# Layer 1: the feed-forward product of a chunk moved among the query heads of a later chunk

## The reference

```python
x = x + _L1_attn_ref(_L1_cond_ref(x, cond), ...)
#   _L1_cond_ref: film of a normed x, 16-head attention of head size 16, W_out
#   _L1_attn_ref: layer norm, 16 query heads of size 128 over one rotated key and value, causal, Wo
x = x + _L1_ffn_ref(_L1_cond2_ref(x, cond), w_fc, w_proj)
#   _L1_cond2_ref: causal depthwise convolution over all 32 lags, taps from cond
h = jnp.maximum(turbo_linear(x, w_fc), 0.0)      # 256 -> 1024
return turbo_linear(h * h, w_proj)               # 1024 -> 256
```

## Time and profile before

| | |
|---|---|
| median of 3 runs | 1476.55 us (1473.99 to 1476.77) |
| profiled execution, span | 1472.0 us |
| PE busy | 1345.4 us, 91% |
| DVE busy | 1101.3 us, 75% |
| ACT busy | 867.2 us, 59% |
| POOL busy | 136.4 us, 9% |
| chain that ended last | PE 49%, DVE 33%, ACT 9%, issue 6% |
| layer 1, steps 1 to 8 | from about 966 us to the end |

### The profile page before, as it was taken

One profiled execution on the slowest core, in us unless ns is written; L12 is line 12 of the kernel. 1 busy time (PEld: TensorE's weight loads), 2 busy tenths in 40 slices (PEclk: granted clock), 3 DMA queues, 4 the chain that ended last, 5 costly groups with the idle time before them and its releaser, 6 DMA issues.

```text
span 1472.0 us, 23108 instructions
## 1 busy us (share of the span) xinstructions
PE 1345.4 (91%) x7939; PEld 966.9 (66%) x7954; DVE 1101.3 (75%) x2860; ACT 867.2 (59%) x1774; POOL 136.4 (9%) x153
## 2 busy tenths in 40 slices
PE   5999998989999999999999967798999999999998
PEld 2444444667787877777777745475767767677766
DVE  4899999758757575757666879768778786969784
ACT  4998899775757576767676573534443434344313
POOL 0000000201010101010101100010210101020100
PEclk9999999999999999999999988998999999999999
DMA  9322233600111010101012310000000000000000
GB/s 379 103 67 66 68 97 84 192 29 29 37 36 44 30 44 30 44 29 44 29 44 82 151 65 8 22 15 1 15 13 11 15 8 22 1 15 8 8 8 15
DMA packets 26523, 73.92 MB, mean 50 GB/s; under 512 B 3992, under 2 KB 5156, under 8 KB 25136
## 3 DMA queue, kind: packets, MB, share of 16 engines
q1 hardware_dynamic: 25840, 71.62, 15.7%
q10 hardware_dynamic: 576, 0.98, 0.2%
HBM read 49.52 MB, written 23.07 MB: 49 GB/s over the span
## 4 chain that ended last, share of the span: by engine, by line
PE 49%; DVE 33%; ACT 9%; issue 6%; DMA 1%; SPq 1%; POOL 0%; DVEq 0%; ACTq 0%
PE psum L613 9%; PE psum L720 7%; PE psum L944 5%; DVE work L1848 4%; DVE ffn_mem L1965 4%; PE psum L659 4%; PE psum L646 4%; DVE h_all L1848 3%; PE psum L983 3%; DVE work L1979 3%; PE psum L973 3%; PE psum L890 2%; PE psum L626 1%; ACT probs_t L1311 1%; PE psum L669 1%
## 5 line engine op out<-in xcount | busy, mean ns | idle before, releaser
L613 PE MATMUL psum<-h_all,w_big 128*128 128x256 f32 x1024 | 244.6, 386 | 4.9 <-ACT work L1269 4.8
L613 PEld LDWEIGHTS psum<-h_all,w_big 128*128 128x128 f32 x1024 | 188.5, 192 | 44.0 <-issue 13.7
L1848 DVE SCALAR_TENSOR_TENSOR work<-work,taps 128x248 f32<-128x248 f32 (+30 forms) x558 | 149.4, 345 | 0.0
L567 PE MATMUL psum<-w_big,h_all 128*64 128x512 f32 x512 | 124.7, 609 | 0.0
L1848 DVE SCALAR_TENSOR_TENSOR h_all<-h_all,taps 128x248 f32<-128x248 f32 (+30 forms) x434 | 117.2, 346 | 1.6 <-DVE h_all L1848 1.6
L944 PE MATMUL psum<-work,w_big 128*128 128x256 f32 x512 | 116.4, 380 | 0.0
L720 PE MATMUL psum<-w_big,gru_mem 128*128 128x256 f32 x512 | 113.6, 379 | 0.5 <-ACT gru_mem L1323 0.5
L720 PEld LDWEIGHTS psum<-w_big,gru_mem 128*128 128x128 f32 x512 | 96.4, 190 | 13.8 <-ACT gru_mem L1323 0.6
L973 PE MATMUL psum<-w_big 128*128 128x256 f32 x448 | 105.3, 388 | 0.0
L944 PEld LDWEIGHTS psum<-work,w_big 128*128 128x128 f32 x512 | 95.5, 190 | 14.8 <-DVE gru_mem L2376 2.5
L1300 ACT ACTIVATE work<-psum 32x128 f32<-32x128 f32 x256 | 68.3, 267 | 53.3 <-PE psum L646 50.8
(11 more groups left out here) (321 smaller groups left out, 2589.9 us busy)
## 6 DMA issues: line engine op xcount, KB each, us to landing
value_rows<-w_emb SPq DMA_DIRECT2D x128, 128.0 KB, 2.3
work<-value_rows SPq DMA_DIRECT2D x16, 1024.0 KB, 5.9
w_big<-in_Wq SPq DMA_DIRECT2D x2, 2048.0 KB, 17.2
w_big<-in_Wo SPq DMA_DIRECT2D x2, 2048.0 KB, 21.5
out<-w_big SPq DMA_DIRECT2D x15, 256.0 KB, 2.0
x_res<-out SPq DMA_DIRECT2D x15, 256.0 KB, 2.7
w_big<-in_Wv SPq DMA_DIRECT2D x1, 2048.0 KB, 18.6
w_big<-in_Wk SPq DMA_DIRECT2D x1, 2048.0 KB, 23.9
```

The source lines that it names most:

```text
L567: mm = pe.matmul(bank(4 + n)[j * B:(j + 1) * B, :], h_all[:, k, :, 2 * pair + j], w_big[:, 2, k * H * HD + n * 512:k * H * HD + (n + 1) * ...
L613: mm = pe.matmul(bank(n % 2)[:, o * TA:(o + 1) * TA], w_big[:, s, k * H * HD + at:k * H * HD + at + HD], h_all[:, k, bass.ds(i * BA, BA), ...
L1848: ins = dve.scalar_tensor_tensor(dst[:, :, lag:], src[:, :, :T - lag], tap, dst[:, :, lag:], ALU.mult, ALU.add)
```

## The change

`fc` of chunks 0 to 5 no longer runs at the end of step i = c + 1. It runs in step c + 2 among the query heads: after heads 2 and 3 tiles 0 and 1, after heads 4 and 5 tiles 2 and 3, and so on. It writes banks 6 and 7 there. Its ReLUs and squares move along, before `keep_cond_turned`. As the convolution of the next chunk starts before `fc` has read the last, its output has two homes. VectorE's order at a step's end becomes lags 10 to 19, layer norm, lags 20 to 25, film, lags 26 to 31, residual. `row_squares` moves ahead of `keep_cond_outputs(ci, 1)` on ScalarE, and three of the last six heads of `rot_project` ahead of the turned rows. The loops over steps 2 to 5 are unrolled. `fc` of chunks 6 and 7 stays where it was.

```diff
-        y3_t = states[:, 512:1024].rearrange("p (k n) -> p k n", k=KD)
+        y3_homes = [area.rearrange("p (k n) -> p k n", k=KD) for area in (states[:, 512:1024], w_big[:, 2, 2048:2560])]
...
-            return x3_buf, x3_t, y3_t
+            return x3_buf, x3_t, y3_homes[c % 2]
+
+        def fc_out(c, f):
+            return bank(f % 2)[:, 0:TA] if c >= NA - 2 else bank(6 + f % 2)[:, 0:TA]
...
-            def fc(c):
-                for f in range(KF):
+            def fc(c, tiles=range(KF)):
+                if 0 in tiles:
+                    pe.wait_ge(conv2_on.sem, 2 * T * c + 2 * T)
+                    if c < NA - 2:
+                        pe.wait_ge(xt2_on.sem, c + 2)
+                for f in tiles:
...
-                    if late:
-                        pe.wait_ge(relu_on.sem, KF * ni)
                     pe.wait_ge(xl_on.sem, i + 1)
...
-                    q_heads(i, range(2, 10))
+                    for h in range(2, 10, 2):
+                        q_heads(i, range(h, h + 2))
+                        if late:
+                            fc(ni - 1, range(h - 2, h))
...
+                    if rot and not begun:
+                        rot_project(i, 1, range(10, 13))
...
-                if ffn:
-                    pe.wait_ge(conv2_on.sem, 2 * T * ni + 2 * T)
+                if ffn and ni >= NA - 2:
                     fc(ni)
...
-                    rot_project(i, 1, range(10, H))
+                    rot_project(i, 1, range(10 if begun else 13, H))
...
-            with pe.Fori(0, NA - 4) as last:
-                chunk1(last + 2, True, True, True, True, True)
+            for i in range(2, NA - 2):
+                chunk1(i, True, True, True, True, True)
...
+                if late:
+                    relus(ni - 1, range(KF))
...
+                if prep and not begun:
+                    row_squares(i + 2)
+                if cond:
                     keep_cond_outputs(ci, 1)
...
-                if ffn:
-                    relu_squares(i - 1, range(0, 2))
+                if late:
+                    relu_squares(i - 2, range(KF))
...
                     if ffn and rot:
+                        if 0 in lags and ni == 1:
+                            dve.wait_ge(y_out, 16)
+                        if 0 in lags and ni >= 2:
+                            dve.wait_ge(fc_sum.sem, KF * (ni - 1))
                         conv(ni, lags, *ffn1(ni)[1:], xt2_on, 1, conv2_on, None)
...
-                    conv2(range(10, T))
+                    conv2(range(10, 20))
                 if cond:
                     layer_norm(ci, clink)
                     c_step.end_trip()
+                if cond:
+                    conv2(range(20, 26))
                 if prep:
                     film_rows(i + 2, lambda ins: link(ins, c_step, i + 2))
+                if cond:
+                    conv2(range(26, T))
```

More of the change, by code:

```diff
@@ L982, in fc @@
                     for k in range(KD):
-                        mm = pe.matmul(bank(f % 2)[:, 0:TA], fc_t[:, k, f * P:(f + 1) * P], ffn1(c)[2][:, k, :],
+                        mm = pe.matmul(fc_out(c, f), fc_t[:, k, f * P:(f + 1) * P], ffn1(c)[2][:, k, :],
                                        start=(k == 0), stop=(k == KD - 1))
@@ L1593, in relus @@
                         act.wait_ge(h2_on.sem, KF * c + f - 1)
-                    act.activation(relu[:, f % 2, :], bank(f % 2)[:, 0:TA], ACT.Relu).then_inc(relu_on.sem, 1)
+                    act.activation(relu[:, f % 2, :], fc_out(c, f), ACT.Relu).then_inc(relu_on.sem, 1)
                     if own_squares(c):
@@ L1656, in chunk1 @@
                     keep_x3(i)
-                if ffn:
-                    relus(ni, range(0, 2))
-                if prep:
+                if ffn and ni >= NA - 2:
+                    relus(ni, range(KF))
+                if begun:
                     row_squares(i + 2)
-                if begun:
                     keep_w5(range(0, 4))
-                if ffn:
-                    relus(ni, range(2, 4))
                 if prep:
@@ L1668, in chunk1 @@
                     keep_w5(range(4, PIECES))
-                if ffn:
-                    relus(ni, range(4, KF))
                 if cond:
@@ L1695, in _ @@
             chunk1(1, True, True, True, True, False)
-            with act.Fori(0, NA - 4) as last:
-                chunk1(last + 2, True, True, True, True, True)
+            for i in range(2, NA - 2):
+                chunk1(i, True, True, True, True, True)
             chunk1(NA - 2, True, True, True, False, True)
@@ L1784, in chunk1 @@
                     hidden_rms(NA - 1, 1)
-                if ffn:
-                    relu_squares(i - 1, range(0, 2))
+                if late:
+                    relu_squares(i - 2, range(KF))
                 if prep:
                     row_rms(i + 2)
-                if ffn:
-                    relu_squares(i - 1, range(2, 4))
                 if cond:
                     norm_rms(i + 1)
-                if ffn:
-                    relu_squares(i - 1, range(4, KF))
             pool.wait_ge(rest_on.sem, GROUPS)
@@ L1818, in _ @@
             chunk1(1, True, True, True, True, False)
-            with pool.Fori(0, NA - 4) as last:
-                chunk1(last + 2, True, True, True, True, True)
+            for i in range(2, NA - 2):
+                chunk1(i, True, True, True, True, True)
             chunk1(NA - 2, True, True, True, False, True)
@@ L2524, in _ @@
             chunk1(1, True, True, True, True, False)
-            with dve.Fori(0, NA - 4) as last:
-                chunk1(last + 2, True, True, True, True, True)
+            for i in range(2, NA - 2):
+                chunk1(i, True, True, True, True, True)
             chunk1(NA - 2, True, True, True, False, True)
```

## The result

The changed kernel takes 1491.09 us (median, 1490.69 to 1491.92) against 1475.27 us of the kernel before, measured beside it: a ratio of 1.0109, 95% interval 1.0096 to 1.0121. It is slower by 1.1%, 15.8 us. 1490.6 was forecast, as 14.0 us on top of 1476.55.

A forecast was written before the change was run, and what follows sets the result against it. The prediction took TensorE to bound layer 1 from end to end. Its terms, +42.1 - 35.3 + 7.2 = +14.0 us on a median of 1476.55, gave 1490.6 us, range 1480 to 1503 us.

The forecast's parts named there:

- `fc` between the seams: Layer 1, TensorE among the query heads of chunks 2 to 7: the moved product adds 6 x 7.01 = +42.1 us.
- seams, 82.9 before: Six stretches from cond_project(ci, 1)'s end to the next conditioning attention (after chunk 6, key product): 82.9 to 47.6, -35.3 us.
- clock: TensorE behind each of six seams: idleness brings a clock drop costing 1.2 us each, +7.2 us.
- Ports: In the seams, GpSimd's norm power beside VectorE's lags: 0 us lost, 2.4 us as the other end.
- The same waits without more clock loss: Rival at the seams: waits as forecast, clock loss no larger than before; +6.8, 1483 us, chance 0.18.
- Two low stretches per seam: Rival behind the seams: two slow-clock stretches each, 20.4 in place of 7.2; +27, 1504 us, chance 0.08.
- The faster case, late lags in half the time: Rival on VectorE: the 24 late lags take half of 4.4 us, no drops; -6.4, 1470 us, chance 0.08.
- stall of `fc` among the heads: Rival among the query heads: ReLUs and squares hold tiles back, adding 10.6 us; 1501 us, chance 0.04.

The follow-up runs named there:

- e3: Changed kernel with VectorE's order norm, film, residual, lags 20 to 31, and ScalarE copying the residual's input before applying the norm: 1461.18 us.
- e4: Changed kernel with seven unneeded products ahead of L893 in chunks 2 to 6, filling TensorE's wait for the residual: 1481.82 us.
- e1: Changed kernel with VectorE's old order at a chunk's end, all lags 10 to 31 before norm, film and residual: 1486.34 us.
- e5: e3 with two more heads of rot_project behind cond_project(ci, 1), eight in place of six: 1460.84 us.
- e7: e3 with ScalarE's copy of the residual's input put behind apply_norm again, as in the changed kernel: 1471.51 us.
- e2: Changed kernel with the conditioning attention's first product writing bank 2, so its wait for the residual falls away: 1474.86 us.

## Why the prediction was right

The forecast rested on three terms. Against the measured ones:

| term | forecast | measured |
|---|---|---|
| `fc` between the seams | +42.1 | +39.1 |
| seams, 82.9 before | 47.6, -35.3 | 47.8, -35.1 |
| clock | +7.2 | +10.0 |
| sum | +14.0 | +14.0 |

The sum is also what the two traces show from the start of chunk 1's seam on: the spans differ by 16.6 us, of which 2.6 lie ahead of it.

- **Seams.** The five that end at L893 were right to 0.06 us, and by the stated path: norm, lags, film, lags, residual. The sixth took 7.71 us in place of 7.27, for the clock fell inside it (the turned x3 took 1.11 us there). e3, which only puts the residual ahead of the lags, takes them from 8.0 to 4.3 us.
- **`fc`.** I said that TensorE never stops among the heads and charged 7.01 us per chunk. Where no drop disturbs it (e4) a chunk takes 61.92 us against 55.41: 6.51. The product's own rate there is 1.727 us for two tiles, 6.91 for eight, and 0.4 us came back: the wait of L970 is 0.28 us where L967 had 0.37, and the other 0.3 stood behind head 9, where TensorE turns the conditioning queries (L906). Before, L906 started 0.52 us after the last pass of head 9, with 0.14 us of waiting for VectorE's L2326; behind `fc` it starts after 0.22 us with none. So "TensorE never stops among the query heads" was not quite true. The unrolled loops and the moved `row_squares` were not run by themselves, but with these two waits the 61.92 us are accounted for, so they have cost nothing here.
- **Clock.** The place was right and the size too small: 6.8 + 2.35 + 2.5 - 1.7 = 10.0. Four drops cost 1.70 us each, which was my upper bound, and the one ahead of chunk 2 cost 2.35. 2.5 us went in chunk 7 (L1043 to the first score 26.60 us, against 17.55 + 6.51). The last term is the last `fc`:

```profile
1452.32 8.86 PE L983 MATMUL psum<-work,ffn_mem 128*128 128x256 f32 x32 [2.57 <-DVE work L1848]
1470.65 7.17 PE L990 MATMUL psum<-work,ffn_mem 128*128 128x256 f32 x32 [2.58 <-DVE work L1853]
```

It has a drop in the profile before (the first line) and none in the changed kernel's. Its wait is 2.56 to 2.58 us in all ten profiles and a drop falls in it in five (before, e1, e4, e5, e7), so this 1.7 us is chance; without it the clock term is 11.7 us. I had taken the price from `fc` in chunks 2 and 3 (1.15 us). There, I take it, part of the loss was hidden behind ReLUs that `fc` waited for in any case; no run isolates that.

- The two errors, -3 and +3 us, cancel. The agreement of the sum is luck to that extent, and so is that of the time to 0.5 us: side by side the medians differ by 15.8 us and not 14.0, and 1490.6 stood on a median of before that was 1.3 us higher than the one measured beside the change.
- **Ports.** Zero was right: lags 20 to 31 took 2.50 + 1.91 = 4.4 us, as forecast, with GpSimd's power beside the first of them. But the row that I gave for it does not show it: that power ended at 884.53 + 0.70 = 885.23 and film began at 885.54, so the two never ran beside each other. A row that does: L2131, a VectorE multiply of two SBUF operands in the kernel before, took its usual 1.23 us at 415.95 beside a power that ran for 5.43 us from 414.55.
- **Rivals.** The same waits without more clock loss is nearly e4 (1481.8; I had said 1483). Two low stretches per seam came true in part, behind two seams of six. The faster case, late lags in half the time, did not come: 4.4 us again. No stall of `fc` among the heads; its price, 1.76 us, was also too high, for it held chunk 3's clock drop (1.15 us).

What I called the intention, to hide the wait for the convolution, did come true: 12.6 us of waits vanished. It was spent on a new wait at the place that the product had covered.

## What to carry to other kernels

A block of work that waits may itself be the cover of everything behind it on the other engines: before moving it, add up the late engine's chain to the next product in the gap that it leaves, and order that chain by who is waited for (here the residual, then `xl`, and the free lags last). Price an idle gap of TensorE with its clock: here 0.92 + 3.42 us of waiting mostly cost 1.7 us more, and work that nobody needed, in the gap, was a net gain. Where a steady chunk gets shorter, look at the first chunk whose cover is missing; e5 gave nearly all of its gain back there.

## What the runs showed that I had not expected

GpSimd and VectorE seem to hold each other up. In GpSimd's timeline of the changed kernel, at the end of chunk 3, and (last line) the same addition in e1:

```profile
1169.92 1.80 POOL L1768 TENSOR_TENSOR stats<-stats,rms_eps 128x2 f32<-128x2 f32 x1 [32.86 <-ACT w_emb L1515]
1171.80 0.70 POOL L1770 TENSOR_TENSOR stats<-stats,minus_half 128x2 f32<-128x2 f32 x1
1175.63 0.71 POOL L1779 TENSOR_TENSOR stats<-stats,minus_half 128x2 f32<-128x2 f32 x1 [3.13 <-DVE stats L2360]
1165.85 2.35 POOL L1768 TENSOR_TENSOR stats<-stats,rms_eps 128x2 f32<-128x2 f32 x1 [32.85 <-ACT w_emb L1515]
```

An addition on two columns (L1768) took 1.80 us; the same addition took 0.20 us in the kernel before, where VectorE was idle beside it (1.80 in each of chunks 1 to 5 here). It began beside the run of lags 10 to 19 and ended at 1171.72, when that run had ended at 1171.67. It looks as if it had waited for the run's end; e1, where the run goes on to 1172.1, shows that it need not: the addition took 2.35 us in two chunks and 2.91 in three, and each time ended in the middle of the run. The power of the same width at 1175.63, beside lags 20 to 25, took its usual 0.71 us; in e1, right behind the addition and beside lags, it took 0.84 to 0.90. The other way round, four lags at 1172.27 in e3 took 2.40 us beside a 1.13 us square of GpSimd and 1.62 us in its chunk 7, where GpSimd was idle; and its 24 late lags took 5.31 us beside another square (1.04 us) and 4.49 ahead of chunk 7, with none. The Trainium skill (SBUF — State Buffer, Who interferes with whom) says that an instruction of VectorE with two SBUF inputs and one of GpSimd that reads SBUF block each other for the whole of one instruction; the lags against the squares agree, 0.8 us longer each time. The addition was held up by more than one lag (each is 0.3 to 0.4 us), and the power hardly or not at all, which that rule does not tell apart. No run isolates it: that this is the ports, and not something else that a run of lags occupies, is argued and not shown.

Whether the clock drops, and for how long, also depended on more than the length of the gap. The same 0.92 + 3.42 us in the changed kernel brought a drop of twice the length at one seam of five. About 3.0 us in one piece in e1 brought the shorter drop at one seam and the longer at three; 0.91 + 1.08 + 0.59 us in e2 cost nothing behind four seams and brought a drop at a fifth. The wait of 2.57 us ahead of the last `fc` brought one in half of the profiles. What decides between them stays open.
